# Second attention by chunks of 512 tokens: q and k parts copied within SBUF into 48 rows on two strips

## The reference

```python
# layer 0: attention (16 heads of 8, 4 kv heads, ALiBi), norm, a linear map through FFTs, norm
# layer 1, attention:
qkv = (x @ W_qkv).reshape(B, S, 3, H, Dh)          # H = 16, Dh = 8
q, k, v = (q[:, :, m], k[:, :, m], v[:, :, m])     # m: rows of 32 tokens, every other row reversed
qs = q.reshape(B, H, nseg, seg, Dh)                # nseg = 8 segments of seg = 128 tokens
ks = k.reshape(B, H, nseg, seg, Dh)[:, :, :, ::2]  # every second key: 64 keys a segment
vs = v.reshape(B, H, nseg, seg, Dh)[:, :, :, ::2]
scores = einsum('bhnqd,bhnkd->bhnqk', qs, ks) * scale
out = einsum('bhnqk,bhnkd->bhnqd', softmax(scores), vs)
y = out (in token order) @ W_out
# layer 1, feed-forward: a mixture of 16 experts around one more attention, norm
```

## Time and profile before

| | us |
|---|---|
| median of 3 runs | 799.55 (799.33 to 804.72) |
| the profiled execution | 806.35 |
| its span, first to last instruction | 804.5 |
| PE busy / DVE / ACT / POOL | 689.3 / 636.0 / 445.1 / 155.7 |
| second attention, first `split` to first `heads_tile` | 403.05 to 481.68 |

### The profile page before, as it was taken

The page is one execution under the profiler, slowest core; times in us unless marked ns, Lnnn a source line. Parts: engine busy times, 40 slices in busy tenths (PEclk is TensorE's granted clock), DMA queues, the critical chain, the costliest instruction groups (busy, mean ns, idle before and its releaser), DMA issues.

```text
span 804.5 us, 16665 instructions
## 1 busy us (share of the span) xinstructions
PE 689.3 (86%) x5878; PEld 441.6 (55%) x5878; DVE 636.0 (79%) x1149; ACT 445.1 (55%) x974; POOL 155.7 (19%) x287
## 2 busy tenths in 40 slices
PE   7499888888888888899955988499999998998883
PEld 5233333333333333335533766499999997996652
DVE  2688999999999999942574647889999994554996
ACT  3058999999999999984641436202111114454442
POOL 6400000000000000003331007601111122123563
PEclk9558999999999999999985669589999998999998
DMA  7711111111111110002556500000000000000000
GB/s 197 222 22 32 32 32 31 32 32 31 33 31 32 32 31 3 2 3 68 142 140 172 156 16 1 0 1 0 2 0 0 0 0 1 0 0 1 15 13 26
DMA packets 19401, 31.87 MB, mean 40 GB/s; under 512 B 4952, under 2 KB 12504, under 8 KB 18040
## 3 DMA queue, kind: packets, MB, share of 16 engines
q1 hardware_dynamic: 17992, 29.42, 13.9%
q0 software_dynamic: 1344, 1.58, 0.7%
HBM read 23.25 MB, written 7.34 MB: 38 GB/s over the span
## 4 chain that ended last, share of the span: by engine, by line
PE 52%; ACT 18%; issue 10%; DVE 10%; DMA 5%; SPq 2%; POOL 2%; DVEq 0%; POOLq 0%; ACTq 0%
ACT probs L1166 16%; PE ps_hi L749 13%; PE ps_lo L998 7%; PE ps_lo L1000 6%; PE ps_lo L999 6%; PE ps_hi L763 4%; PE ps_hi L1058 3%; DMA q_rep<-mrow 2%; DVE probs L1747 2%; DVE mx L1465 2%; PE ps_hi L1049 1%; SPq L385 1%; ACT mrow L1121 1%; PE ps_hi L810 1%; PE ps_hi L930 1%
## 5 line engine op out<-in xcount | busy, mean ns | idle before, releaser
L1465 DVE TENSOR_REDUCE mx<-ps_lo 128x2 f32<-128x1024 f32 x256 | 306.2, 1224 | 12.2 <-PE ps_lo L726 9.0
L1166 ACT ACTIVATE probs<-ps_hi 128x512 f32<-128x512 f32 x512 | 278.0, 596 | 38.4 <-PE ps_hi L749 25.8
L763 PE MATMUL ps_hi<-probs,v_blk 128*32 128x256 f32 x2048 | 168.2, 401 | 5.6 <-ACT mrow L1121 5.5
L749 PE MATMUL ps_hi<-q,k 28*128 28x512 f32 x512 | 132.0, 509 | 26.9 <-ACT probs L1166 13.0
L726 PE MATMUL ps_lo<-k,q 26*128 26x512 f32 x512 | 135.7, 526 | 7.0 <-DVE mx L1465 4.2
L1681 DVE SCALAR_TENSOR_TENSOR tok_cur<-ps_lo,w_cur,tok_cur 128x384 f32<-128x384 f32 x240 | 127.6, 608 | 6.3 <-PE ps_lo L1000 4.7
L749 PEld LDWEIGHTS ps_hi<-q,k 28*128 28x128 f32 x512 | 49.5, 187 | 139.5 <-ACT probs L1166 117.7
L998 PE MATMUL ps_lo<-w_hi,op_hi 128*128 128x384 f32 (+1 forms) x304 | 108.1, 356 | 19.8 <-DVEq L1642 10.1
L999 PE MATMUL ps_lo<-w_lo,op_hi 128*128 128x384 f32 (+1 forms) x304 | 105.4, 347 | 0.0
L1000 PE MATMUL ps_lo<-w_hi,op_lo 128*128 128x384 f32 (+1 forms) x304 | 105.4, 347 | 0.0
L763 PEld LDWEIGHTS ps_hi<-probs,v_blk 128*32 128x32 f32 x2048 | 42.3, 109 | 72.5 <-ACT probs L1166 58.5
(11 more groups left out here) (225 smaller groups left out, 842.8 us busy)
## 6 DMA issues: line engine op xcount, KB each, us to landing
q<-q_parts SPq DMA_DIRECT2D x30, 192.0 KB
q_rep<-q_parts SPq DMA_DIRECT2D x8, 576.0 KB
k<-k_parts SPq DMA_DIRECT2D x32, 96.0 KB
k_rep<-k_parts SPq DMA_DIRECT2D x24, 96.0 KB
q_parts<-qk_hi SPq DMA_DIRECT2D x8, 256.0 KB, 4.9
q_parts<-qk_p SPq DMA_DIRECT2D x12, 128.0 KB, 3.1
xa<-in_L_attn_x SPq DMA_DIRECT2D x4, 256.0 KB, 3.9
q_parts<-qk_lo SPq DMA_DIRECT2D x4, 256.0 KB, 6.3
```

Of the source, the lines that this page charges most:

```text
L749: mm = pe.matmul(bank(4 + (2 * n + a) % 3), k0[rows, k_at:k_at + P], q0[rows, h * QN:(h + 1) * QN], start=True, stop=True)
L763: mm = pe.matmul(o_bank()[32 * r:32 * r + 32, 0:OW], v_all[:, at:at + 32], probs0[:, n % P_RING, r * OW:(r + 1) * OW], start=(kb == 0), st ...
L1166: act.activation(probs0[:, n % P_RING, a * QN:(a + 1) * QN], bank(4 + (2 * n + a) % 3), ACT.Exp).then_inc(s0_free, 1)
L1465: dve.reduce_max(mx2[:, j % 2, :, i, kh], bank(2 * (m % 2), 2).rearrange("p (a n) -> p a n", a=2), AX_X).then_inc(max0_done, 1)
```

## The change

A score is now the sum of six pairs of parts (`PART_PAIRS`) instead of nine: 48 rows. The heads are dealt to two strips of partitions, 0 to 47 and 64 to 111 (even heads on the first, odd ones on the second), so that a step s is one chunk of 512 tokens and half of the heads on both strips; steps 2q and 2q+1 belong to chunk q. `q_rep` and `k_rep1` hold all four chunks, there is no ring. The parts go from `qk_p` straight into the rows, SBUF to SBUF: for each chunk twelve DMAs of 8 x 8 x 512 on SP (`load_q1`) and twelve of 8 x 8 x 256 on POOL (`load_k1`), six pairs on two strips each. The HBM scratch tensors and their stores are gone. `load_mrow` has four DMAs a step instead of two.

So that the 64 q columns of a strip lie in the order that the copies need, the q and k columns of the layer's weights are permuted once: they are loaded into `w_stage`, and two copies on POOL put them in order. ACT takes over `seg_o` from DVE, and `heads_tile` needs two transposes a tile instead of four.

```diff
+PART_PAIRS = ((0, 0), (0, 1), (0, 2), (1, 0), (1, 1), (2, 0))
+ROWS = len(PART_PAIRS) * DH
...
-            def load_rep(s):
...
+            def load_q1(q):
+                for part in range(PARTS):
+                    sp.wait_ge(part_set[part], q + 1)
+                    for i in copies_of(part, 0):
+                        for strip in range(2):
+                            sp.dma_start(q_rep[copy_rows(strip, i), q * HP * QN:(q + 1) * HP * QN]
+                                         .rearrange("d (h n) -> d h n", n=QN),
+                                         qk_p[HALF * strip:HALF * (strip + 1), q, part, 0:QN]).then_inc(q1_in[q], 16)
...
-            for dst, src in ((wo_sb, wo), (w_qkv1, w_qkv), (wout_sb, w_out), (sim_sb, sim), (rank_sb, rank)):
+            for dst, src in ((wo_sb, wo), (wout_sb, w_out), (sim_sb, sim), (rank_sb, rank)):
                 sp.dma_start(dst[:], src).then_inc(ld_w1, 16)
+            sp.dma_start(w_qkv1[:, 2 * D:W3], w_qkv[:, 2 * D:W3]).then_inc(ld_w1, 16)
+            sp.dma_start(w_stage, w_qkv[:, 0:2 * D]).then_inc(ld_w1, 16)
...
+            for q in range(NQ - 1):
+                load_q1(q)
             load_mrow(0)
+            load_q1(NQ - 1)
+            for s in range(1, NS):
                 load_mrow(s)
...
             blocks(NS * KB, NT * 8)
+
+            pool.wait_ge(ld_w1, 6 * 16)
+            for n in range(2):
+                at = slice(n * D, (n + 1) * D)
+                pool.tensor_copy(w_qkv1[:, at].rearrange("p (s d h) -> p h s d", s=2, d=DH),
+                                 w_stage[:, at].rearrange("p (h s d) -> p h s d", s=2, d=DH)).then_inc(w1_set, 1)
 
             for j in range(NH):
                 pool.wait_ge(mx_all_set, j + 1)
...
-            fill(k_rep1[64:96, :].bitcast(words), two_ones)
+            for strip in range(2):
+                r0 = HALF * strip + ROWS // 32 * 32
+                fill(k_rep1[r0:r0 + 32, :].bitcast(words), two_ones)
...
-                if q >= 2:
-                    parts1_stored(dve, q)
...
-            def seg_o(s):
-                dve.wait_ge(seg_p_free, s + 1)
-                dve.tensor_copy(o_seg[:, s * 512:(s + 1) * 512], bank(6 + s % 2)).then_inc(seg_o_free, 1)
```

More of the change, by code:

```diff
@@ L56 @@
 K_EXP = ROWS + 2
-RING = 4
 STEPS = KB * HG
@@ L61 @@
 W3 = 3 * D
-K_STORES = (1, PARTS)
 WC, NWC = 1024, 8
@@ L278, in parts0_stored, with copies_of, copy_rows @@
             engine.wait_ge(k_out[0][q % 2], q // 2 * PAIRS * 16)
-        def parts1_stored(engine, q):
-            engine.wait_ge(q_out[1][q % 2], q // 2 * PARTS * 16)
-            engine.wait_ge(k_out[1][q % 2], q // 2 * PARTS * 16)
+        w_stage = attT[:, 0, 0:2 * D]
+        def copies_of(part, side):
+            return [i for i, pair in enumerate(PART_PAIRS) if pair[side] == part]
+        def copy_rows(strip, i):
+            return slice(HALF * strip + i, HALF * strip + ROWS, len(PART_PAIRS))
         block = ctx.enter_context(nc.Block())
@@ L489, in store_k0, with load_k1 @@
                                    part[0:G * DH, q % 2, QN:2 * QN].bitcast(F32)).then_inc(k_out[0][q % 2], 16)
[L491 to L498, removed]
+            def load_k1(q):
+                for part in range(PARTS):
+                    pool.wait_ge(part_set[part], q + 1)
+                    for i in copies_of(part, 1):
+                        for strip in range(2):
+                            pool.dma_start(k_rep1[copy_rows(strip, i), q * HP * KN:(q + 1) * HP * KN]
+                                           .rearrange("d (h n) -> d h n", n=KN),
+                                           qk_p[HALF * strip:HALF * (strip + 1), q, part, QN:QN + KN]
+                                           ).then_inc(k1_in[q], 16)
             def root(n, q):
@@ L799, in heads_tile @@
                     pe.wait_ge(ot_read, t - 7)
-                for g in range(G):
-                    mm = pe.transpose(bank(t % 8)[:, g * P:(g + 1) * P], source(t, g), ident_sb[:])
+                for f in range(2):
+                    mm = pe.transpose(bank(t % 8)[:, f * P:(f + 1) * P], source(t, f), ident_sb[:])
                 mm.then_inc(ot_ps, 1)
@@ L885, in _, with seg_at, seg_max @@
                 v_products(q)
-            def seg_max(s, h):
-                slot = s % RING
-                n = s * (HG + 2) + h
-                if n >= 2:
[L893 to L898, removed]
+            def seg_at(s, h, g):
+                at = (s // 2 * HP + s % 2 * HG + h) * QUAD + g
+                return slice(at * SEG, (at + 1) * SEG), slice(at * KSEG, (at + 1) * KSEG)
+            def seg_max(s, step):
+                n = s * (HG + 2) + step
+                if n >= 2:
+                    pe.wait_ge(seg_max_done, n - (step > 0))
+                rows = slice(HALF * (step % 2), HALF * (step % 2) + K_MAX)
+                for h in range(2):
+                    for g in range(QUAD):
+                        q_at, k_at = seg_at(s, step // 2 * 2 + h, g)
+                        c = (h * QUAD + g) * KSEG
+                        mm = pe.matmul(bank(step % 2)[:, c:c + KSEG], q_rep[rows, q_at], k_rep1[rows, k_at],
+                                       start=True, stop=True)
                 mm.then_inc(seg_max_ps, 1)
@@ L1243, in _ @@
                                    bank(2 + 2 * f, 2), ACT.Exp).then_inc(seg_s_free, 1)
+                if s:
+                    seg_o(s - 1)
+            seg_o(NS - 1)
             act.wait_ge(ld_we, 4 * 16)
@@ L1434, in split @@
                 dve.wait_ge(ksel_sb, q + 1)
-                if q >= 2:
-                    parts1_stored(dve, q)
-                parts = [qk_p[:, q % 2, i, 0:n] for i in range(PARTS)]
+                parts = [qk_p[:, q, i, 0:n] for i in range(PARTS)]
                 link(dve.tensor_copy(parts[0], qk[:, 0:n]))
```

141 lines of the change are left out of this document (54 added, 87 removed).

## The result

| | us |
|---|---|
| changed kernel, median of 20 runs | 805.33 |
| kernel before, median of 20 runs beside it | 800.17 |
| ratio, 95% interval | 1.0066 [1.0041, 1.0091] |
| profiled execution of the changed kernel, its span | 803.49, 801.7 |
| second attention in it, first `split` to first `heads_tile` | 404.53 to 481.56 |

The ratio is +5.3 us of 800, against +4.8 predicted. A second measurement of the same kernel gave 1.0060 [1.0027, 1.0092].

What follows compares the result with a forecast made beforehand. The prediction took the second attention to hang on SP's queue and landings, the first on a fixed rhythm of DVE, PE and ACT. 5.8 - 0.7 - 0.3 = +4.8 us gave a median of 804.4 us, range 795 to 812.

Steps and rivals of the forecast that it cites:

- Part 1: First attention's start: POOL's wait for the weights and two copies delay the first `mx_parts`, +5.8 us (bounds +2.8 to +6.9).
- Part 2: SP's queue in the second attention: 36 loads at 0.632 us precede four `mrow` rows; T0 431.1, T1 -0.8 us.
- T0: Time at which PE starts the scores of step 0 in the second attention: forecast 431.1, before 431.17.
- T1: Time at which PE starts the scores of step 1 in the second attention: forecast 441.1, -0.8 us; before 441.95.
- Part 3: Second attention's steps: two of 6.2 us at half clock, then 5.4 each; -0.7 us in all, tail -0.3 us.
- T7: Time at which PE starts the scores of step 7 in the second attention: forecast 475.1, before 475.81.
- Part 4: Covered edits: second `k_rep1` fill fits POOL's idle time, POOL's 48 k loads take 25.5 us, a chunk ahead of PE.
- Dear issues: Rival: SP's issues cost p = 0.826 us each, T1 10.7 us late, 815.5; 1% passed from p = 0.66; chance 0.14.
- Half of the DMA engines: Rival: second attention's loads use eight of sixteen engines, T1 some 5 us late, about 809 us; chance 0.12.
- Cheap issues: Rival: SP's issues cost p = 0.364 us each, T1 falls to about 435, 7 us less, 797.5; chance 0.14.
- Clock: Rival: PE at full clock from T1 on in the second attention, all six steps 5.4 us, 801.6; chance 0.07.
- Delay not there: Rival: the delay at the first attention's start shrinks to +2.8 us, 801.4, inside the forecast's range; no separate chance.

Runs made afterwards that it cites:

- experiment 2: Kernel before plus only the staged weight load, POOL's wait and two copies ahead of its head loop: 810.06 us, ratio 1.0066 to the kernel before.
- experiment 1: Changed kernel with POOL's wait for the weights and its two copies moved behind the head loop: 800.30 us, ratio 0.9968 to the kernel before.
- experiment 4: Changed kernel with the edits of experiment 1 and experiment 3 together: 800.45 us, ratio 0.9941 to the kernel before.
- experiment 6: experiment 5 with POOL's wait and two copies put back ahead of the head loop: 797.65 us, ratio 0.9952 to the kernel before.
- experiment 3: Changed kernel with `mrow` rows moved up in SP's queue, between the q loads: 801.94 us, ratio 0.9988 to the kernel before.
- experiment 5: experiment 4 with 28 of the 80 DMAs issued by ACT: 790.69 us, ratio 0.9890 to the kernel before; repeated, 791.76 us, 0.9870.

## Why the prediction was right

Forecast +4.8 us, measured +5.3 with an interval of 3.3 to 7.3. Its two parts were measured apart, and both have the sign and the place that were forecast: the wait by experiment 2 (+0.66% or +5.3 us, forecast +5.8), the second attention by experiment 1 (-0.32% or -2.6 us, forecast -1.0). Together these make +2.7 us, and the whole measured +5.3; the intervals of the parts, 2 to 3.5 us to either side, are wide enough for that, but the closeness of 4.8 to 5.3 is better than the parts are known, and in part luck.

**Part 1, +5.8 us.** The place and the mechanism are as forecast. In the trace the delay is 7.0 us: the load was issued at 37.56, not 37.2, its 128 KB landed after 7.6 us, not 7.0, and the copies took 0.67, not 0.6. All three small errors have one sign, and the result lies just above the bound of +6.9, which had counted the same landing and dearer copies but the earlier issue. Over all thirteen profiles the first `mx_parts` is at 38.3 us on average where nothing is waited for (eight) and at 45.8 where it is (five), 7.5 us apart. At the last `big` copy the same groups are at 371.0 and 374.9, 3.9 apart (4.8 without experiment 4, whose profile has the lowest clock, 0.913), with single executions scattered over 10 us. So part of the delay comes back in the traces, where the prediction had said that a delay is "not caught up anywhere" and had allowed 1.6 us at most; its sign "all later heads some 6 us late" did not come true in the profile. The prediction let the end of the half-clock stretch move along with the work. In the profiles PE was at half clock for 39.6 us on average where the wait is and 39.3 where it is not (between 18 and 98 us), so on average the wait did not lengthen the stretch, though single profiles lie between 27 and 58. By the prediction's own alternative that gives back (13.4 - 9.6) / 13.4 of the 7.5 us, 2.1 us as an estimate. How much stays is only bracketed: 5.3 us (experiment 2), 5.2 to 6.6 (experiment 6), 4 to 5 in the traces, and 0.0098 or some 8 us by ratios between the change and experiment 1, which were not measured beside each other.

**Part 2, T0 and T1.** The term that was mis-sized is the price of a load: 0.632 us was counted, the queue took 0.68 on average and then 0.66. Counted from SP's first issue, the 36 loads took 24.52 us and not 22.8 (+1.7), and T0 came 29.6 us behind it, forecast 27.4. For T1 twelve more loads added 0.4, and the landing, 1.74 us in the chain above where 2.82 was taken, gave 1.1 back: T1 is 38.75 us behind the first issue, forecast 37.4, and 38.3 before. So +0.5 in place of -0.8. "Gains **nothing**, because `load_q1`(1) and (2) are queued ahead of `mrow`" held: experiment 3 puts chunk 2 behind `mrow`, and T0 comes 6.2 us earlier.

**Part 3.** Two steps of 6.2 us at half clock, set by PE, and then steps of 5.4, set by the rows, were forecast, 34.0 us from T1 to T7. Measured are 32.3: three steps of 5.7, one of 5.5, and two of 4.9 and 4.8 that ran in part at the higher clock. The sum is near, but its reason was not: after T1 PE waited for rows at three steps only (0.23, 0.65 and, at the last, 2.67 us), and most steps were set by PE at half clock, as from 443.98 to 449.68, with no wait. A step at half clock is shorter than 6.2, because the blocks of `seg_max` take 0.82 us and not 1.03; the prediction had counted no gain there ("a product's time shows columns, not rows"). `seg_scores`, with 50 rows where there were 74, still took 1.06. From T0 to T7 it is 41.4 us, 44.6 before and 44.0 forecast. The gain to the transposes is 1.6 us in the profiles (0.2 in the repeat of the change, whose distance is 110.0) and 0.2 to 4.9 by the ratio of experiment 1; 1.0 was predicted.

**Part 4.** POOL never came last: its 48 loads took 28.31 us from 405.44 on, and no wait of PE ends with one. The fills of `k_rep1` end 0.64 us ahead of the next root; the cover held, with little left (timeline of POOL):

```profile
375.41 7.08 POOL L452 MEMSET k_rep<- 32x4096 uint32 x2
383.13 1.05 POOL L490 TENSOR_TENSOR rstd<-ve,half 128x4 f32<-128x4 f32 x1 [0.64 <-DVE ve L1483]
```

**Rivals.** *Dear issues* came part of the way: from the 0.588 taken, p rose to 0.612, a third of the way to the 0.66 from which 1% was reckoned, and by the mean of all 48 loads (0.678 with its gap, so 0.634) nearly two thirds; shorter landings and a cheaper `seg_max` stood against it. *Half of the DMA engines*: the view of the DMA queues of the changed kernel from 408 to 430 us (q1 carries SP's loads, q0 POOL's; packets, MB, share of sixteen engines):

```profile
q1 hardware_dynamic: 2264, 2.06, 32.2%
q0 software_dynamic: 1183, 1.20, 22.2%
```

Together they take 54.4% of sixteen engines' time, more than eight engines have, so not all of it ran on the same eight: the form of the rival that was priced at 809 is refuted. SP's loads alone take 32.2%, so eight would suffice for them, and `mrow` landed in 1.7 us, 3.1 at most: no transfer was late, since the issues were the slower part. Which engines they used no row shows. The rule of the Trainium skill ("DMA: Bandwidth & Descriptors", section "Why a DMA increments its semaphore by 16 and not by 1"), by which such a load runs on eight, is thus neither shown nor refuted for a single load; no cost of it is seen here. *Cheap issues*: no load was near 0.364. *Clock*: the six last steps were not all at the full clock, and the mean of the window 430:480 was 0.64; but the clock moved single executions more than the change did. *Delay not there*: the load landed after 7.6 us, not 4.0, and experiment 2 (+1.8 to +8.7 us) and experiment 6 show a price.

What the forecast missed is how near a clearly faster kernel was: the loss came from the place of one wait and the gain was held back by the order of one queue, and with both mended (experiment 5) the same rewrite is 1.2% below the kernel before.

## What to carry to other kernels

Preparation for a late stage belongs where its engine is idle, not where it is written most easily: a wait for a load ahead of an in-order loop delays it by the landing of the load, 7 us here, and the whole program pays most of it (4 to 8 us), while the same copies 300 us later went into time that POOL had to spare. When loads are cut finer, count the issues of each queue and what stands behind them; the small rows that the critical path needs must not queue behind bulk loads for later chunks, and an engine with slack can issue some of them, though an issue took longer while both were at it (0.93 and 0.83 us for 0.66). Judge each part by itself before judging the sum: here -0.3% and +0.7% stood against each other.

## What the runs showed of the hardware

- **Landing within SBUF**: rows of `mrow`, 4 KB a DMA, landed in 1.7 us (median) where the same view of the kernel before has 2.2/3.1/6.8 for 8 KB, with loads from HBM beside them. With two queues issuing (experiment 5) it has 1.7/2.1/5.7, in the repeat 1.7/2.3/6.3.
- **Maxima products**: sixteen products of 64 columns, eight on one strip of 48 rows and then eight on the other, took 0.82 us at half clock; on one set of 72 rows they took 1.03. Rows and strips changed together, and no run tells them apart.
- **The clock's share of the scatter**: in the runs of one kernel the time goes with the mean granted clock. In the changed kernel 0.930 goes with 801.4 to 804.0 us, 0.926 with 803.5 to 805.0, 0.922 with 805.7 to 808.0, 0.918 with 809.0 to 809.6. How long PE stays at its lower clock at the start of the first attention differed from profile to profile: by windows of 2 us from 18 to 98, 34 us and 48 us in the two profiles of the change itself, and 27 to 58 us over all thirteen. I found no edit that sets it; in the second attention (404 to 490) it is 51 us in experiment 4 and 44 with spare products, 31 and 41 in experiment 5 and 33 with them, so those did not clearly set it either. That stays open, and with it how much of a delay of 7.5 us remains at the end, between 4 and 8.
